# A two-pass attention and expert network on one core: expert weights stationary instead of the rows, batch 1 joined early, new engine orders

## The reference, cut to what matters

```
gate = silu(rows @ Wg[e])      # 256 -> 176
up   = rows @ Wu[e]            # 256 -> 176
out  = (gate * up) @ Wd[e]     # 176 -> 256
x    = x + weight * out        # for both experts of the row
```

## Time and profile before

| what | us |
|---|---|
| median of 3 runs (500.54 to 500.78) | 500.75 |
| span of the profiled execution, first to last instruction | 499.1 |
| what the runs' median has beyond that span | 1.65 |
| TensorE busy | 448.1 |
| VectorE busy | 364.7 |
| ScalarE busy | 271.1 |
| GpSimd busy | 249.9 |

### The profile page before, as it was taken

How to read it: one execution, slowest core, us unless ns; L and a number is a source line. 1 busy time by engine, 2 the same in 40 slices (tenths; PEclk the granted TensorE clock), 3 DMA queues, 4 the chain that set the end, 5 groups by cost and what they waited for, 6 DMA issues and landing times.

```text
span 499.1 us, 11100 instructions
## 1 busy us (share of the span) xinstructions
PE 448.1 (90%) x3401; PEld 311.1 (62%) x3401; DVE 364.7 (73%) x1066; ACT 271.1 (54%) x654; POOL 249.9 (50%) x309
## 2 busy tenths in 40 slices
PE   6999999999999999999999859889688999999950
PEld 3546667677666676667777626465566767777640
DVE  6899989989899875953445648788898685444563
ACT  4579899998887965333333424835234433433310
POOL 6409559129843063674334566248575676333340
PEclk9999999999999999999999997999979999999995
DMA  5664710110321243464335394102224466333685
GB/s 191 240 237 188 172 42 6 62 34 15 115 77 44 86 129 118 128 202 138 106 106 161 79 193 66 43 2 94 77 86 127 150 187 193 121 106 96 187 279 189
DMA packets 43736, 60.80 MB, mean 122 GB/s; under 512 B 5856, under 2 KB 38240, under 8 KB 43040
## 3 DMA queue, kind: packets, MB, share of 16 engines
q1 hardware_dynamic: 33152, 37.74, 25.2%
q0 software_dynamic: 9984, 21.83, 14.4%
q10 hardware_dynamic: 544, 0.52, 0.3%
HBM read 28.91 MB, written 25.00 MB: 108 GB/s over the span
## 4 chain that ended last, share of the span: by engine, by line
PE 57%; DVE 27%; issue 5%; DMA 5%; ACT 3%; POOL 2%; SPq 0%; DVEq 0%; ACTq 0%
PE PS L1195 15%; PE PS L1215 10%; DVE qa L1570 7%; PE PS L1083 5%; PE PS L1059 4%; PE PS L1207 3%; PE PS L1185 3%; PE PS L1258 3%; DVE n_stat L1474 2%; PE PS L1225 2%; DMA kbd<-ys 2%; PE PS L1101 2%; PE PS L1085 2%; PE PS L1134 2%; PE PS L1061 2%
## 5 line engine op out<-in xcount | busy, mean ns | idle before, releaser
L1961 POOL DMA_INDIRECT ys<-yo,xin x78 | 76.1, 976 | 90.5 <-DVE yo L1781 80.3
L1195 PE MATMUL PS<-wexp,xTt 128*128 x312 | 105.7, 463 | 1.9 <-DVE yo L1781 1.1
L1570 DVE TENSOR_REDUCE qa<-PS 128x1 f16<-128x512 f32 (+3 forms) x176 | 101.8, 636 | 5.8 <-PE PS L1061 5.2
L1384 ACT ACTIVATE prob<-PS 128x512 f16<-128x512 f32 (+1 forms) x176 | 91.7, 564 | 8.7 <-PE PS L1085 7.2
L1946 POOL DMA_INDIRECT xs<-xn,pos x64 | 62.7, 980 | 59.4 <-DVE pos L1655 43.2
L1215 PE MATMUL PS<-wexp,hT 88*128 x312 | 79.0, 382 | 2.2 <-ACT hT L1434 2.1
L1768 DVE SCALAR_TENSOR_TENSOR sg<-th,PS 128x176 f32<-128x176 f32 x78 | 26.2, 335 | 68.8 <-ACT th L1428 67.5
L1195 PEld LDWEIGHTS PS<-wexp,xTt 128*128 128x128 f32 x312 | 54.0, 190 | 21.0 <-issue 3.0
L1083 PE MATMUL PS<-qT,kbd 128*128 128x512 f16 (+3 forms) x256 | 62.0, 299 | 0.8 <-ACT prob L1384 0.5
L1215 PEld LDWEIGHTS PS<-wexp,hT 88*128 88x128 f32 x312 | 54.8, 190 | 11.9 <-issue 3.4
L1059 PE MATMUL PS<-kbd,qT 128*128 128x512 f16 (+1 forms) x176 | 59.9, 360 | 2.6 <-DVE qa L1570 1.8
(11 more groups left out here) (215 smaller groups left out, 796.4 us busy)
## 6 DMA issues: line engine op xcount, KB each, us to landing
xin<-xs SPq DMA_DIRECT2D x78, 129.0 KB, 2.3
wexp<-in_experts SPq DMA_DIRECT2D x4, 1216.0 KB, 9.7
kbd<-ys SPq DMA_DIRECT2D x18, 256.0 KB, 4.3
xs<-zeros SPq DMA_DIRECT2D x32, 129.0 KB
xn<-xn SPq DMA_DIRECT2D x8, 512.0 KB, 3.3
xall<-ys POOLq DMA_DIRECT2D x6, 512.0 KB, 6.9
out<-xall SPq DMA_DIRECT2D x8, 256.0 KB, 2.8
kbd<-kT SPq DMA_DIRECT2D x60, 32.0 KB, 1.8
```

The costliest lines, as they stand in the source:

```text
L1195: mm = pe.matmul(PS[:, bank, 0:2 * FI], xTt[:, j % NXT, kc * P:(kc + 1) * P], wexp[:, bass.ds(expert[f, j], 1), kc * 2 * FI:(kc + 1) * 2 * FI]
L1384: act.activation(prob[:, u % NPR, 0:nr * w], PS[:, bank, 0:nr * w], ACT.Exp, scale=ATT_SCALE)\
L1570: dve.tensor_reduce(qa[:, b % 2, i, REP * g + r0:REP * g + r0 + nr, HD], PS[:, bank, 0:nr * w].rearrange("p (r w) -> p r w", r=nr), AX.X, ...
L1961: pool.indirect_dma_start(ys[f], bass.IndirectOffsetOnAxis(xin[:, j % NXIN, D + 1:D + 2].bitcast(I32), axis=0), yo[:, j % NYO], None).then ...
```

## The change

Gate and up swap operands. The 352 columns are laid out as three stationary chunks: gate columns 0 to 127, up columns 0 to 127, and a third of 112 that holds the last 48 of gate, 16 columns of padding, and the last 48 of up from position 64. The turned rows (128 columns) move. The result comes out already turned, hidden units on partitions, so `hidden`, its transposes and its ScalarE copy are gone. Since a stationary operand is read here from a fixed place, a new ScalarE step `weights` copies the expert's 736 columns into one of two homes, which lie over attention buffers (`xh`/`xhT` and `prob`). The first copy waits for the last projection of attention, and copy j for `gate_up` of tile j-2.

`JOINED` gets batch 1 of the first pass: its rows are fetched by SyncE and added by VectorE. `NUDGE` becomes a far longer list, keyed also by the second index or by the stage, several step costs are new, and the orders with them. `cT` now lies over `oT`.

```diff
-JOINED = [(0, 0)] + [(1, b) for b in range(B)]
+JOINED = [(0, 0), (0, 1)] + [(1, b) for b in range(B)]
...
-         ("bank_shift",): 204,
+         ('bank_shift',): 887.1, ('banks',): -74.5,
...
-("plan", 0): 89
+('plan', 0): 1548.7
...
+        wgu = (xhs[:].rearrange("p n s -> p (n s)").bitcast(F32)[:, 0:DOWN],
+               prob[:].rearrange("p n s -> p (n s)").bitcast(F32)[:, KC * P:KC * P + DOWN])
...
                     elif kind == "gate_up":
                         f, j = a
-                        if j == 0 and f == 0:
-                            pe.wait_ge(experts_loaded, 16 * NE // 2)
+                        pe.wait_ge(weights_ready, TILES * f + j + 1)
...
-                        for kc in range(KC):
-                            mm = pe.matmul(PS[:, bank, 0:2 * FI], xTt[:, j % NXT, kc * P:(kc + 1) * P],
-                                           wexp[:, bass.ds(expert[f, j], 1), kc * 2 * FI:(kc + 1) * 2 * FI]
-                                           .rearrange("p a f -> p (a f)"), start=(kc == 0), stop=(kc == KC - 1))
+                        for c, (lo, rows) in enumerate(CHUNKS):
+                            for kc in range(KC):
+                                mm = pe.matmul(PS[0:rows, bank, c * P:(c + 1) * P],
+                                               wgu[j % 2][:, kc * GU + lo:kc * GU + lo + rows],
+                                               xTt[:, j % NXT, kc * P:(kc + 1) * P], start=(kc == 0), stop=(kc == KC - 1))
...
-                    elif kind == "hidden":
...
-                        for c in range(2):
-                            mm = pe.transpose(PS[0:FH, bank, c * P:(c + 1) * P], hf[:, j % 2, c * FH:(c + 1) * FH],
-                                              ident_f)
...
+                        for c, rows in enumerate((P, REST)):
+                            mm = pe.matmul(PS[:, bank, 0:D], hT[0:rows, j % 2, c],
+                                           wexp[0:rows, bass.ds(expert[f, j], 1), DOWN + c * D:DOWN + (c + 1) * D]
...
+                    elif kind == "weights":
...
+                        if f == 0 and j == 0:
+                            act.wait_ge(experts_loaded, 16 * NE // 2)
+                            made(act, "project", B - 1, 1)
+                        if j >= 2:
+                            made(act, "gate_up", f, j - 2)
+                        act.activation(wgu[j % 2], wexp[:, bass.ds(copied_expert[f, j], 1), 0:DOWN]
+                                       .rearrange("p a f -> p (a f)"), ACT.Copy).then_inc(weights_ready, 1)
...
-                        dve.tensor_tensor(hf[:, j % 2], sg[:, j % 2], PS[:, bank, FI:2 * FI], ALU.mult)\
+                            made(dve, "down", f, j - 2)
+                        dve.tensor_tensor(hT[:, j % 2, 0], sg[:, j % 2, 0], PS[:, bank, P:2 * P], ALU.mult)
+                        dve.tensor_tensor(hT[0:REST, j % 2, 1], sg[0:REST, j % 2, 1],
+                                          PS[UP:UP + REST, bank, 2 * P:3 * P], ALU.mult)\
```

More of the change, by code:

```diff
@@ L90 @@
 OUTPUT_BANKS = (5, 6)
[L95 to L133, removed]
@@ L136 @@
+TILE_KINDS = ("load", "xT", "weights", "gate_up", "down")
 class Work:
@@ L393, in norm @@
                [(DVE, "mem_out", b, 2 * n), (DVE, "mem_out", b, 2 * n + 1)])[s]
[L394 removed]
+        w.add(DVE, r(), 1.15, "stats", s, b, n, after=src + ([(POOL, "pow", *last), (DVE, "scale", *last)] if last else []), behind=[(DVE, "stats", s, b, 0)] * n)
     w.add(POOL, r(), 1.03, "pow", s, b, after=[(DVE, "stats", s, b, n) for n in range(2)]
@@ L422, in route @@
     t = r()
-    w.add(PE, t, 0.75, "router", f, b, after=[(ACTE, "turn", 2 * f, b, kc) for kc in range(KC)], banks=banks,
+    w.add(PE, t, 0.6, "router", f, b, after=[(ACTE, "turn", 2 * f, b, kc) for kc in range(KC)], banks=banks,
           emptied=(ACTE, "router", f, b))
@@ L447, in release @@
     if n == LAST:
-        w.add(SP, rank, 9.0, "pads", f, after=[(DVE, "plan", f, n, 2)], lands=2.5)
+        w.add(SP, rank, 5.0, "pads", f, after=[(DVE, "plan", f, n, 2)], lands=2.5)
 def tile(w, f, j, rank, gap, banks):
@@ L460, in tile @@
     follow = lambda e, kind: [(e, kind, f, j - 1)] if j else []
-    w.add(SP, t(-4), 0.45, "load", f, j, after=src + used, behind=follow(SP, "load"), lands=2.3)
+    w.add(SP, t(-4), 0.4, "load", f, j, after=src + used, behind=follow(SP, "load"), lands=2.3)
     w.add(PE, t(-1), 0.22, "xT", f, j, after=[(SP, "load", f, j)] + follow(PE, "xT"), banks=banks["X"],
@@ L478, in tile, with copies @@
     w.add(POOL, t(2), 1.26, "down", f, j, after=[(DVE, "down", f, j)], behind=follow(POOL, "down"), lands=2.5)
+def copies(w, f, j, rank, gap):
+    w.add(ACTE, rank - gap, 0.68, "weights", f, j, after=[(DVE, "plan", f, stage_of(j), 2), (SP, "load_experts")]
+          + ([(PE, "gate_up", f, j - 2)] if j >= 2 else [(PE, "project", B - 1, 1)]))
 def tile_before(f, j, n):
@@ L539, in memory @@
         t = NT * b + i - 2
-        w.add(PE, times[i + 1], 0.89, "combT", b, i, after=[(POOL, "main", b, i, kc) for kc in range(KC)], banks=(3, 4),
+        w.add(PE, times[i + 1], 0.5, "combT", b, i, after=[(POOL, "main", b, i, kc) for kc in range(KC)], banks=(3, 4),
               emptied=(ACTE, "combT", b, i))
@@ L595, in plan_work @@
         rest = (1, 2) if j < LEAD else (2, 3, 4) if j < STAGES[LAST][1] else (2, 3, 4, 7)
-        tile(w, 0, j, rank, 3, {"X": rest, "G": (0, 1)[:1 + (j >= LEAD)], "H": rest, "Y": rest})
+        copies(w, 0, j, rank, 3)
+        tile(w, 0, j, rank, 3, {"X": rest, "G": (0, 1)[:1 + (j >= LEAD)], "Y": rest})
     start = tail + 20 + 3 * MIXED
@@ L608, in plan_work @@
         rest = (3, 4, 5, 6) if j < STAGES[LAST][1] else (3, 4, 5, 6, 7)
-        tile(w, 1, j, last + 3 * j, 3, {"X": rest, "G": (1, 2), "H": rest, "Y": rest})
+        copies(w, 1, j, last + 3 * j, 3)
+        tile(w, 1, j, last + 3 * j, 3, {"X": rest, "G": (1, 2), "Y": rest})
     for b in range(B):
```

246 lines of the change are left out of this document (195 added, 51 removed), and 4 rows, old and new, of the table NUDGE.

## The result

The changed kernel takes 525.89 us (median of 5 runs, 521.93 to 528.73) against 500.78 for the kernel before on the same chip: a ratio of 1.0471, 95% interval 1.0424 to 1.0518 (the two medians alone give 1.050). One of the five runs of the kernel before took 1553.53 us and is left out of the ratio; the other four took 500.54 to 501.48. Forecast were 489.7 us and a range of 478 to 499. The profiled span is 520.1 us against 499.1 before: 21.0 more, and 32.0 more than the 488.1 that the sum gave for the span.

What follows compares the result with a forecast made beforehand. TensorE was taken to bound the expert passes, VectorE the memory block from 300, both VectorE and ScalarE nearly full in attention. Span 499.1 - 6.3 - 0.7 + 4 - 4 - 4 = 488.1, time 489.7 us, range 478 to 499.

Steps and rivals of the forecast that it cites:

- The step that failed: TensorE in each expert tile: `down` keeps 4 instructions of 256 columns and its 0.86 us despite the new row split.
- Those on the load: Two rivals on TensorE's weight loads: they set its pace (557.0 us, chance 0.03) or aren't hidden at all (649, 0.01).
- The 12 matmuls: `gate_up` in each expert tile: 12 matmuls of 128 moving columns at 0.11 us each, 1.32 together.
- ScalarE and VectorE per tile: Expert tiles: ScalarE 1.55 us and VectorE 1.46 fit under TensorE's 2.40, so the term is 0.
- 31 tiles x 0.09: First expert pass: TensorE saves 0.09 us on each of 31 tiles, part of the -6.3 over 70 tiles.
- the start (+4): First expert pass: the first tile waits for attention's last projection and starts at 183.1, costing 4 us (0 to +8.3).
- VectorE's work (-4): Attention: bank constants and first plan move behind attention's reduces on VectorE, gaining 4 us (0 to -7.4).
- -4 was forecast between tile 30 and the second pass: Memory block: joining batch 1 early moves its norm and two products into VectorE's idle stretch, -4 us (0 to -8.1).
- 39 x 0.09 = -3.5: Second expert pass: TensorE saves 0.09 us on each of 39 tiles, part of the -6.3 over 70 tiles.
- -0.7 was forecast: Behind the last `gate_up`: transposes and their copy leave the tile's chain, saving 0.7 us (0 to -1.2).
- The later start costs more than the orders give: Rival: first tile loses all 8.3 us, neither attention nor batch 1 gains; 502.0 us, chance 0.09.
- TensorE's saving doesn't arrive: Rival, expert tiles: matmul spacing of 0.117, scatters or holes eat TensorE's saving; 496.0 us, chance 0.13.

Runs made afterwards that it cites:

- 128 rows: The changed kernel with the second `down` operand raised from 48 to 128 stationary rows, the added rows zero: 508.12 us, ratio 1.0138 to the kernel before.
- fill-in run: 128 rows plus SyncE load and fetch edits and PSUM bank edits, with 25 idle-time matmuls added in TensorE's waits ahead of the second pass: 504.64 us, ratio 1.0066.
- the last run: The fill-in run's kernel with VectorE's batch 0 joins moved behind later tiles' products and batch 3's fetches issued ahead of two stores: 502.57 us, ratio 1.0025.

## Why the prediction was wrong

**The step that failed** is "`down` keeps 4 instructions of 256 columns, 0.86 (128 and 48 rows instead of 88 and 88)". It set the split of 128 and 48 equal to that of 88 and 88. It cost 1.15, and 0.10 more in the `gate_up` behind it: 0.39 a tile. In the span this is 15.0 us (520.1 - 505.1; 17.8 by the medians), not 70 x 0.39 = 27, since the slower tiles cover waits that show with 128 rows, such as that for tile 38's load (5.7 between two `gate_up` there, 3.0 in the changed kernel). No rival had it. Those on the load spoke of full loads at every pass; this one is a gap at two places in a tile.

**The 12 matmuls were right:** 1.33 with 128 rows against 1.32, and a tile of 2.41 against 2.40. The reading of the earlier trace rows, that full loads hide behind 128 columns, held.

**ScalarE and VectorE per tile were right.** The copy is 816 ns (0.79), tanh 383 (0.38), `sg` 420 (0.42), the products 287 and 290 (0.28 each). TensorE doesn't wait for the copy in the steady state.

**The other 17.0 us** (505.1 against 488.1, so with the failed step undone) split by the table:

- *Up to tile 30: 5.5.* 31 tiles x 0.09, the start (+4) and VectorE's work (-4) made -2.8; it was +2.7. The first tile was expected at 183.1, and 182.65 came. But the sum takes VectorE's -4 off beside that, so it needed 179.1, and 3.5 are lost there: attention's last projection came 5.7 earlier (180.71) instead of the 7.9 that its tail (3.9) and VectorE (4) were to give, and the first `gate_up` 1.9 behind it instead of 0.6. The other 2.0 are recovery: the tiles were 7.9 late at the first, 4.2 at tile 9 and 2.7 at tile 30's scatter, 5.1 of the 7.1 forecast. The one PSUM bank is not shown to be the cause, since other banks gave no lasting gain and the first tiles came as far apart before; that it is batch 3's routing on VectorE and ScalarE is argued only.
- *Memory block: 5.1.* -4 was forecast between tile 30 and the second pass; it was +1.1 (113.9 against 112.9). Batch 1's norm comes at 287.8 instead of 301.7, and the block's products on VectorE take 62.9 us instead of 75.5. But they start 6.5 later. 2.7 of it is tile 30, and 1.3 is batch 1's first join (283.04 to 284.37), which stands ahead of the norm of batch 0's second half in VectorE's queue. The order of the fetches isn't the cause, by the run that changed it, and the rest isn't traced. Behind the products 15.6 us pass to the first `gate_up` instead of 5.6, because GpSimd's scatters and the row loads now end last. VectorE was the bound of the block, and with its products done 6.1 earlier the next engine was.
- *Second pass: 5.8.* 39 x 0.09 = -3.5 was forecast from first to last `gate_up`; it was +2.3 (100.7 against 98.4). The load behind four fetches was 2.5 of it (98.2 with the load moved). A lower clock at the start was about 1, by the fill-in run's sixth tile. With the join moved as well, the last run has 94.8: the saving was there, and these waits had hidden it.
- *The end: 0.6.* -0.7 was forecast, -0.1 came; behind the last `gate_up` stand fetches, adds and stores.

With the last edits the span is still 12.7 above the sum: 10.7 ahead of the second pass (382.57 where the terms make 371.9), and the rest behind its last `gate_up`.

Of the rivals, the one on the slow side, "The later start costs more than the orders give" (502.0), is nearest to what 128 rows gave (508.12), but only in part for its reason: the first tile is 7.9 late (8.3 there), but attention's end did move, and 2.7 of the 7.9 are left at tile 30. "TensorE's saving doesn't arrive" (496.0) had the orders gain 8, and the saving per tile did arrive once the rows were 128.

## What to carry to other kernels

A split of the stationary operand is not priced by its instructions and columns alone: look whether its row count changes from one load to the next, and, where one is 64 or fewer beside full ones, fill up with zero rows or split evenly. The sign is a load that idles for "issue" in each tile together with a longer distance between the starts of the matmuls. And before a gain in one stage is added to the sum, name the engine that ends the next stage; here GpSimd's scatters and the row loads took back what VectorE's part of the memory block gave.

## What was not expected of the hardware

- Between stationary operands of 128 (or 88) and of 48 or 64 rows the next weight load isn't hidden: 0.39 us a tile (2.80 against 2.41), and 0.34 in the kernel before (2.83 against 2.49), for one change each way. 128 beside 96 or 88 rows costs nothing that can be seen; between 64 and 88 nothing was measured.
- Where TensorE had idled ahead of the second pass, its granted clock was 0.80 over 375 to 400, and the first 12 matmuls took 2.77 us; with 25 matmuls in the waits it was 1.00 and 1.49.
